# Wide attention layers of a four-block kernel: finer waits for the scores, bias scores of both signs on ScalarE, and another order of projections at each layer's start

## The reference, cut to what matters

```
h      = layernorm(x)                        # 512 rows
q,k,v  = h @ wq + bq, ctx @ wk + bk, ctx @ wv + bv      # 16 heads of 128
k,v    = concat(k, bias_k), concat(v, bias_v)           # one more key and value per head
x      = x + softmax(q k^T / sqrt(128)) v @ wo + bo
```

## Time and profile before

| | us |
|---|---|
| median of 3 runs | 1091.75 (1088.05 to 1092.27) |
| the profiled execution, its time | 1090.92 |
| its span, first to last instruction | 1089.1 |
| PE busy | 952.1 (87%) |
| DVE busy | 777.3 (71%) |
| ACT busy | 604.8 (56%) |
| POOL busy | 312.8 (29%) |
| mean granted TensorE clock | 0.944 of full |

### The profile page before, as it was taken

How to read it: one execution, slowest core, us unless ns; L and a number is a source line. 1 busy time by engine, 2 the same in 40 slices (tenths; PEclk the granted TensorE clock), 3 DMA queues, 4 the chain that set the end, 5 groups by cost and what they waited for, 6 DMA issues and landing times. The chain is left out here.

```text
span 1089.1 us, 17930 instructions
## 1 busy us (share of the span) xinstructions
PE 952.1 (87%) x6616; PEld 807.3 (74%) x6616; DVE 777.3 (71%) x1627; ACT 604.8 (56%) x1369; POOL 312.8 (29%) x321
## 2 busy tenths in 40 slices
PE   4888886789999999998899999998588899779958
PEld 4766665679988898987688989888467666556657
DVE  3486766458877887886678878777683688667864
ACT  3587873236555555553355556555443788267842
POOL 3454540050221122221111222200004456345510
PEclk8899998999999999998899999999878899889989
DMA  4996006140110011111000111000213940394020
GB/s 149 268 233 88 2 2 230 31 147 1 39 39 4 37 40 39 40 39 39 1 4 37 40 39 39 2 1 1 74 47 111 232 63 2 98 236 70 4 84 20
DMA packets 39490, 72.71 MB, mean 67 GB/s; under 512 B 6534, under 2 KB 23944, under 8 KB 37228
## 3 DMA queue, kind: packets, MB, share of 16 engines
q1 hardware_dynamic: 39404, 71.56, 24.7%
HBM read 55.28 MB, written 16.27 MB: 66 GB/s over the span
## 5 line engine op out<-in xcount | busy, mean ns | idle before, releaser
L1312 ACT CAST L1a_probsT_hi<-L1a_bank 128x512 fp32r<-128x512 f32 x128 | 68.8, 590 | 94.3 <-PE L1a_bank L1190 94.3
L1148 POOL TENSOR_SCALAR L1a_wo_hi<-L1a_stage 128x512 fp32r<-128x512 f32 x16 | 10.4, 651 | 362.4 <-PE L1a_sums L74 355.2
L1346 ACT ACTIVATE L1a_probs<-L1a_scores,L1a_neg_max 128x512 f32<-128x512 f32 x128 | 87.0, 685 | 30.9 <-DVE L1a_bias_shifted L1435 26.0
L1431 DVE TENSOR_REDUCE L1a_top<-L1a_scores 128x2 f32<-128x1024 f32 x64 | 78.2, 1223 | 34.7 <-PE L1a_scores L74 34.6
L1369 DVE TENSOR_TENSOR L1a_probsT_lo<-L1a_bank,L1a_probsT_hi 128x512 fp32r<-128x512 f32 x128 | 82.0, 682 | 0.1
L72 PE MATMUL L1a_bank<-L1a_probsT_hi,L1a_v_hi 128*128 128x256 f32 x256 | 73.1, 286 | 9.2 <-DVE L1a_probsT_lo L1369 9.2
L1314 ACT ACTIVATE L1a_attended_hi<-L1a_bank,L1a_cols 128x256 fp32r<-128x256 f32 x64 | 30.5, 476 | 90.3 <-PE L1a_bank L74 90.3
L72 PE MATMUL L1a_bank<-L1a_w_hi,ctxT_hi 128*128 128x256 f32 x256 | 75.8, 296 | 1.1 <-DVE L1a_k_lo L1371 1.1
L417 POOL TENSOR_SCALAR L0a_probs<-L0a_probs,L0a_inverse 128x768 f32<-128x768 f32 x64 | 57.4, 909 | 57.9 <-DVE L0a_inverse L686 57.9
L73 PE MATMUL L1a_bank<-L1a_w_lo,ctxT_hi 128*128 128x256 f32 x256 | 73.2, 286 | 0.0
L74 PE MATMUL L1a_bank<-L1a_w_hi,ctxT_lo 128*128 128x256 f32 x256 | 73.1, 286 | 0.0
(11 more groups left out here) (410 smaller groups left out, 3095.9 us busy)
## 6 DMA issues: line engine op xcount, KB each, us to landing
L1a_stage<-in_L_w SPq DMA_DIRECT2D x15, 1024.0 KB, 4.8
L0m_fold_wq<-in_L_wqT SPq DMA_DIRECT2D x2, 2048.0 KB, 13.0
L0a_k_dram<-L0a_kT_hi SPq DMA_DIRECT2D x8, 384.0 KB, 10.3
L0a_k_stack<-L0a_k_dram SPq DMA_DIRECT2D x4, 576.0 KB
L0a_w_qkv<-L0a_k_dram SPq DMA_DIRECT2D x4, 576.0 KB
L0a_wide_wo<-in_L_wo SPq DMA_DIRECT2D x1, 2048.0 KB, 16.6
L0a_wide_wo<-in_L_wo SPq DMA_DIRECT2D x2, 1024.0 KB, 17.6
L0m_stage<-in_L_wm SPq DMA_DIRECT2D x4, 512.0 KB, 6.3
```

The lines of the kernel that those rows point to most:

```text
L1312: nc.scalar.copy(out, source).then_inc(ring.hi_done, 1)
L1346: nc.scalar.activation(probs[:, g % 2, qt, :], scores[:, qt, :], ACT.Exp, bias=neg_max[:, g % 2, qt:qt + 1], accum_out=row_sum[:, g % 2, q ...
L1431: link(nc.vector.tensor_reduce(top[:, :], scores[:, :, :], AX.X, ALU.max))
```

## The change

- Each unit's `score` waits only for its own queries and keys: the first unit of a pair for q0 and k00, the second for k01, the third for q1 and k10, the fourth for k11. The wait for the values moves to `product_v`, in the two units of the pair's first head, two waits each. The wait of the first `score` of a layer for the bias scores is gone.
- ACT writes both `bias_scores` and `neg_bias_scores` from PSUM; DVE's negation goes, and DVE waits for a new semaphore.
- At a layer's start the order is q0, bias scores, q1.
- In the second layer six projections stand ahead of the norm's transposes in place of four (PE, ACT and DVE alike). DVE takes the low parts of the first two between the statistics and `apply`.
- In the second layer POOL waits, behind the root, until `apply` is done, before it writes `wo` of that pair.

```diff
@@ -1049,8 +1049,10 @@
             return shared[what]
 
         FIRST = KV + ["norm0", "norm1"]
-        START = ["norm0", "norm1"] + KV + QS + ["bias_scores"]
-        AGAIN = KV[:4] + ["norm0", "norm1"] + KV[4:] + QS + ["bias_scores"]
+        LAST = [QS[0], "bias_scores", QS[1]]
+        NORM_AT = 6
+        START = ["norm0", "norm1"] + KV + LAST
+        AGAIN = KV[:NORM_AT] + ["norm0", "norm1"] + KV[NORM_AT:] + LAST
         job_of, n = {}, 0
         for item in START:
             job_of[(0, item) if item in PROJ else (item, 0)] = n
@@ -1092,6 +1094,7 @@
         pool_done, w_ready, wo_ready = ph.sem("pool_done"), ph.sem("w_ready"), ph.sem("wo_ready")
         cols_scaled, out_done, scores_full = ph.sem("cols_scaled"), ph.sem("out_done"), ph.sem("scores_full")
         max_done, exp_done, normed, dve_done = ph.sem("max_done"), ph.sem("exp_done"), ph.sem("normed"), ph.sem("dve_done")
+        bias_scored = ph.sem("bias_scored")
         sums_full, sums_free = ph.sem("sums_full"), ph.sem("sums_free")
         first_loaded = [ph.sem(f"first_loaded{c}") for c in range(4)]
         first_hi, first_lo, ones_set = ph.sem("first_hi"), ph.sem("first_lo"), ph.sem("ones_set")
@@ -1142,6 +1145,7 @@
                     pool.wait_ge(first_loaded[3], 16)
                 if p == PAIRS + 1:
                     parts[1].root(nc, pool)
+                    pool.wait_ge(parts[1].normed_ready, 1)
                 if p >= 2:
                     pool.wait_ge(out_done, UN * (p - 1))
                 part = stage[j][:, 1536:2048]
@@ -1194,6 +1198,9 @@
             def product_v(g):
                 j, hh, b, h = unit(g)
                 job = job_of["V", g]
+                if hh == 0:
+                    for t in range(b * SK, (b + 1) * SK, 2):
+                        ring.wait_evacuated(pe, job_of[g // UN, ("v", t)])
                 ring.wait_evacuated(pe, job_of["T", g, 0])
                 ring.wait_evacuated(pe, job_of["T", g, 1])
                 ring.wait_bank(pe, job)
@@ -1235,8 +1242,7 @@
                 ring.wait_evacuated(pe, job_of["norm1", layer])
                 if layer == 0:
                     pe.wait_ge(first_lo, 3)
-                for item in QS:
-                    project(p, item)
+                project(p, QS[0])
                 job = job_of["bias_scores", layer]
                 ring.wait_bank(pe, job)
                 pe.wait_ge(cols_scaled, LAYERS)
@@ -1248,6 +1254,7 @@
                                          start=kt == 0, stop=False)
                     last = nc.tensor.matmul(out, ones[:, :], bias_product[layer][:, :], start=False, stop=True)
                 last.then_inc(ring.full, 1)
+                project(p, QS[1])
 
             for layer in range(LAYERS):
                 if layer:
@@ -1258,18 +1265,15 @@
                     if n in (0, 4) and layer == 0:
                         pe.wait_ge(first_lo, 1 if n == 0 else 2)
                     project(PAIRS + 1 if layer else 0, item)
-                    if n == 3 and layer:
+                    if n == NORM_AT - 1 and layer:
                         parts[layer].transpose(nc, pe, ring, keep)
                 queries(layer)
                 for gl in range(GL + 1):
                     g = layer * GL + gl
                     p, u = divmod(g, UN)
                     if gl < GL:
-                        if u == 0:
-                            for item in PROJ:
-                                ring.wait_evacuated(pe, job_of[p, item])
-                            if gl == 0:
-                                ring.wait_evacuated(pe, job_of["bias_scores", layer])
+                        for item in ((QS[0], KV[0]), (KV[1],), (QS[1], KV[2]), (KV[3],))[u]:
+                            ring.wait_evacuated(pe, job_of[p, item])
                         score(g)
                     if gl:
                         transposes(g - 1)
@@ -1325,15 +1329,16 @@
                 for n, item in enumerate(KV):
                     p = p0 + 1 if layer else 0
                     high(job_of[p, item], destination(p, item)[0], bias_of(p, item))
-                    if n == 3 and layer:
+                    if n == NORM_AT - 1 and layer:
                         parts[layer].scale(nc, act, ring)
                 act.wait_ge(cols_scaled, LAYERS)
-                for item in QS:
-                    high(job_of[p0, item], destination(p0, item)[0], bias_of(p0, item))
+                high(job_of[p0, QS[0]], destination(p0, QS[0])[0], bias_of(p0, QS[0]))
                 job = job_of["bias_scores", layer]
                 act.wait_ge(ring.full, job + 1)
-                nc.scalar.mul(keep["bias_scores"][:, :, :].rearrange("p t h -> p (t h)"), ring.bank(job)[:, 0:RT * H],
-                              scale).then_inc(ring.hi_done, 1)
+                for what, by in (("bias_scores", scale), ("neg_bias_scores", -scale)):
+                    last = nc.scalar.mul(keep[what][:, :, :].rearrange("p t h -> p (t h)"), ring.bank(job)[:, 0:RT * H], by)
+                    last.then_inc(bias_scored if by > 0 else ring.freed_by(job), 1)
+                high(job_of[p0, QS[1]], destination(p0, QS[1])[0], bias_of(p0, QS[1]))
                 for gl in range(GL + 1):
                     g = layer * GL + gl
                     p, u = divmod(g, UN)
@@ -1394,7 +1399,11 @@
                         last = nc.vector.tensor_tensor(keep["x"][:, t, :], sums[:, t, :], keep["x"][:, t, :], ALU.add)
                     last.then_inc(sums_free, 1)
                     dve.wait_ge(sums_free, layer)
-                parts[layer].normalise(nc, dve, link, keep["x"], 1e-5, True)
+                parts[layer].statistics(nc, link, keep["x"], 1e-5, True)
+                if layer:
+                    for item in KV[:2]:
+                        low(job_of[p0 + 1, item], destination(p0 + 1, item), bias_of(p0 + 1, item))
+                parts[layer].apply(nc, dve, keep["x"], True)
                 if layer == 0:
                     for n, c in enumerate(FIRST_ORDER[:3]):
                         low_weights(n + 1, c)
@@ -1409,18 +1418,15 @@
                     dve.wait_ge(ones_set, 2)
                 for n, item in enumerate(KV):
                     p = p0 + 1 if layer else 0
-                    low(job_of[p, item], destination(p, item), bias_of(p, item))
-                    if n == 3 and layer:
+                    if n >= 2 or not layer:
+                        low(job_of[p, item], destination(p, item), bias_of(p, item))
+                    if n == NORM_AT - 1 and layer:
                         split_norm(layer)
                 dve.wait_ge(cols_scaled, LAYERS)
                 for item in QS:
                     low(job_of[p0, item], destination(p0, item), bias_of(p0, item))
-                job = job_of["bias_scores", layer]
-                highs[0] += 1
-                dve.wait_ge(ring.hi_done, highs[0])
-                last = nc.vector.tensor_scalar(keep["neg_bias_scores"][:, :, :], keep["bias_scores"][:, :, :], -1.0, None, ALU.mult)
-                last.then_inc(ring.freed_by(job), 1)
-                ring.wait_evacuated(dve, job)
+                dve.wait_ge(bias_scored, layer + 1)
+                ring.wait_evacuated(dve, job_of["bias_scores", layer])
                 for gl in range(GL + 1):
                     g = layer * GL + gl
                     p, u = divmod(g, UN)
```

## The result

The kernel after takes 1071.66 us (median of 4 runs, 1071.27 to 1073.68) against 1089.92 of before, timed beside it: a ratio of 0.9837, interval 0.9818 to 0.9855. Its profiled execution took 1073.68, its span is 1071.9. The prediction said 1072, with a span of 1070.1.

What follows compares the result with a forecast made beforehand. PE was taken to set the pace, so its waits were priced: 10.4 + 6.1 + 2.5 = 19.0 us off 1091.75 gives 1072.7, stated as 1072. Own bounds about 1067 to 1077, range 1064 to 1080.

Steps and rivals of the forecast that it cites:

- Pair starts: At a pair's first score, 11 PE stops of 0.89 us vanish in full: 9.8 us, 10.4 with two further pair starts.
- ten met waits in a row: At two pair starts without a DVE stop, the waits themselves cost some 0.4 us each; 0.6 us gain for both.
- Opening of layer two: Norm transposes' 3.15 us stop, 2.8 of slow clock and the 2.85 stop go; first scores 519.5 instead of 528.06.
- at full clock: In layer two's opening, the 0.50 clock at 510 to 516 goes with the norm's stop, worth 2.8 us.
- The hold at the second score: POOL's w_lo holds DVE's small instructions in a layer's first unit; second score comes 7.1 us behind the first.
- Layer one: At layer one's start the 2.75 us stop goes; gain 2.5 us, 4.3 if DVE isn't held, 1.3 if the clock falls.
- The phases behind: Phases after the wide layers begin at a barrier and shift as a whole: 0 us.
- the four steps: Pair starts 10.4, layer two's start 6.1 (opening and first pair together), layer one's start 2.5: 19.0 us.
- The first: Rival: the pair-start stop only moves to a wait for a bank behind the score; 1083 us, chance 0.05.
- the fourth: Rival: DVE isn't held at the layer starts, 4.0 + 1.8 us more gain; 1067 us, chance 0.08.
- The second: Rival: layer starts give half, the opening keeping its stop and the clock staying low; 1077 to 1078 us, chance 0.09.
- The third: Rival: added waits on PE delay DVE, line 1435 is held behind w_lo in 12 pairs; 1100 us, chance 0.06.

Runs made afterwards that it cites:

- e1: Kernel before with the finer waits alone (scores wait for their own queries and keys, values' waits in product_v): 1081.43 us against 1088.91, ratio 0.9914.
- e7: Kernel after with twelve more long-met waits ahead of each first-head product with v, from the second pair on: 1074.67 us, ratio 0.9867.
- e2: Kernel before with the norm's part alone (six projections ahead of its transposes, two low parts before apply, POOL behind apply): 1085.51 us, ratio 0.9964.
- e3: Kernel before with the bias part alone (ACT writes both signs, order q0, bias scores, q1, first score not waiting for them): 1086.67 us, ratio 0.9980.
- e6: Kernel after without POOL's wait for apply: 1072.87 us, ratio 0.9861.
- e4: Kernel after, with POOL's w_hi and w_lo of pairs 2 and 10 held until the exponentials of the layer's first unit are done: 1078.87 us, ratio 0.9907.
- e5: Kernel after with the bias scores back behind both query projections (q0, q1, bias scores), ACT still writing both signs: 1067.65 us, ratio 0.9808.
- e11: Kernel after, unchanged, run again: 1074.90 us, ratio 0.9851.
- e12: The kernel of e5, unchanged, run again beside e11: 1068.73 us, ratio 0.9800.
- e8: The kernel of e5 with eight of the twelve small matmuls of layer two's bias scores left out: 1066.41 us, ratio 0.9775.
- e10: The kernel of e5 with bias scores behind each layer's first scores and, in layer one, POOL's key and value weights released earlier: 1067.44 us, ratio 0.9782.

## Why the prediction was right, step by step

**Pair starts: right.** The stop was priced at 0.89 and gave 0.82 to 0.91 in each of 11 pairs, 9.7 us for the 9.8 of the sum, and nothing was late behind it; e1 shows the same alone. The term "ten met waits in a row" (0.6 for two pair starts) came to some 0.8, but its reason was wrong: e7 shows twelve met waits at no cost. The pair starts at 269.47 and 747.32, put down to "issue", stand 0.26 and 0.29 us behind the end of a low part of the values (the one at 267.93, 1.28 long, ends at 269.21), and the stops at 301.98 and 334.49 stand 0.25 and 0.26 behind theirs: it was the same stop, cut short. The table's 9.9 is less than these 10.5, as the gain of 0.3 at 269.47 counts in layer one's first pair, and as the last pair of layer two, where PE waits for the transposes' low parts, got 0.35 longer (30.06 to 30.41), which the sum had not asked about.

**Opening of layer two: the stop right, the clock 1.2 us too much and in part luck.** The stop of 3.15 and the slow clock behind it went (e2 alone: 5.9 us), `apply` took 1.37 (1.4 to 1.6 said), the transposes had no stop. What failed is the step "at full clock" up to the first scores: the clock fell at 509, without a pause of PE, and the second query projection took 2.59 us instead of 1.38. The sum also took the 2.8 us of slow clock as what the stop costs; the same stop has 6.8 us of low clock behind it in before, 3.4 in e3 and none in e1, so that term was read from one execution, and the 7.40 of the two traces holds up to 2.3 that the edit did not earn. Also unforeseen: POOL's wait gives next to nothing (e6). A slip without weight: the transposes' start less the stop is 507.2, not 507.0.

**The hold at the second score: right.** The second score was said 7.1 us behind the first and came 7.23 behind it in both layers, with the hold in both, and the cold second unit after it in layer two alone. By the Trainium skill, SBUF — State Buffer, section "Who interferes with whom", a DVE instruction with two SBUF inputs contends with a GpSimd instruction that reads SBUF, the form of L1439 included; the trace agrees with 2.48 and 2.02 us on that line and 0.16 on the next. Layer two's first pair lost 2.0 where 2.5 was taken: the first unit 1.1 for 0.9, the cold second one 0.8 and the third 0.1 for 1.5. e4 and e5 show POOL as the cause from both sides, and e4 that its work, moved later, holds other instructions of DVE.

**Layer one: 3.2 for 2.5.** The stop of 2.75 went and 0.8 came by chance: PE's stop at the value projections, set by the arrival of weights, was 1.08 before and 0.28 after, and e1, with the order of before, has none and a is 0.8 shorter there. In e7 it is 0.7, and in e5 it is absent, but the clock is at 0.50 until 222.9, where in the kernel after it is back at 219.0; a is 20.35 in both. The first pair lost 0.39 where 0.3 was taken, by a balance: its second unit took 0.6 longer, and its fourth 0.3 less, without the stop at 269.47.

**The phases behind took 1.7 us more,** which nothing in the change touches, with the clock low for as long (67.6 and 67.8 us); the cause is open. It cancels chance gains ahead (0.45 and 0.8). So the total is as near as it is in part by luck: the four steps summed to 19.0, the wide part gave 18.5, of which 0.8 is not of the change and up to 2.3 more is a slow stretch of before's trace that e1, with the same stop, does not have.

**Rivals.** The first and the fourth have no row: no stop moved to a bank, and small instructions were held. The second had one half right, the clock, but by another cause. The third's price was near (31 us for 28, by the size alone) and its trigger wrong: the forecast stands some 0.2 us of DVE's time from a cliff of 3%, and waits on PE don't bridge it.

## What to carry to other kernels

A wait for more than the next instruction needs costs its stop once per loop, and the gain of narrowing it can be read off before: stop plus restart, if what is next late has slack. Where two engines hold each other at SBUF, moving the one can move the hold to another instruction, and a short instruction more can lose a place in front of a long one: look at the order of starts, in tenths of a microsecond, in every unit. A slow stretch behind a stop is worth a second trace before it goes into a sum: here the same stop came with 6.8, 3.4 and 0 us of it. Independent work that stands ahead of the critical instruction can fill the idle stretch behind it instead (here the bias scores, moved behind the first scores); that kernel had the shortest wide part of all that compute the whole.

## What the runs showed of the hardware

**The clock falls behind small matmuls that leave PE no pause.** PE worked on 12 matmuls of 16 columns (24 rows of the trace, 2.7 us) with a busy share of 1.00, and the granted clock went from 1.00 to 0.50, that is to 1.2 GHz, between 0.5 us before their end and 1.0 behind it, for 3.4 us. In layer two it did so in all eight traces in which PE goes on without a stop behind the full twelve: the kernel after (509.2), e11 (509.7), e5 (509.6), e12 (510.7), e6 (511.0), e7 (511.9), e4 (514.2) and e3 (522.2). In layer one of the same eight it did so in e12 alone, so these matmuls are not enough by themselves, and what else it takes is not shown. It did not with 4 of the 12 (e8), nor with the 12 behind the first scores (e10), one trace each. The Trainium skill, TensorE: Matmul & The Clock Gate, section "HAM oscillation", ties the fall to idle gaps; the stretches behind 3.85 us (after) and 3.36 us (e8) of idle agree, the stretch at 509 to 512 shows it without one.

**The same stop does not bring the same clock.** At the stop ahead of the norm's transposes (3.15 us in before, 3.14 in e3, 3.13 in e1) the clock fell to 0.50 in before and stayed there for 6.8 us, in e3 for 3.4 us, and in e1 it did not fall. Stops of 1.63 (layer one, after), 1.03 (e10) and 1.99 us (e4, 521.17) were followed by no fall, one of 1.83 (e5, 516.20) was.

**What the clock brings to a whole run** is as large as a part of this change: e1's executions lie between 1075.80 and 1085.45.

**POOL's hold is not for one form alone.** Beside POOL's work on `wo` stood L760 (4 in 3.09 us, 1.37 alone), and beside that on `w_hi` and `w_lo`, at different times, a small two-input instruction (2.48 us, 0.16 alone) and the normalisation (2 in 4.04, 0.88 alone), all held; the reduce, which reads PSUM, was not (1.21 to 1.23 throughout).
